# Third block's rows loaded first; low halves of w2 after the last indirect store; first expert weights loaded ahead of the expert stage

## The reference, cut to what matters

```python
h = _layernorm(x) * (1 + ca) + sa
x = x + ga * attention(h)              # causal; scores = tanh(qk) + two bias terms
h = _layernorm(x) * (1 + cb) + sb
logits = silu(h @ rw1 + rb1) @ rw2 + rb2
k_prob = softmax(top_k(logits, 2))
for e in range(8):
    out += we[:, None] * (silu(h @ w1[e] + b1[e]) @ w2[e] + b2[e])
x = x + gb * out
```

## Time and profile before

| | before |
|---|---|
| runs | 1859.3, 1864.91, 1857.8 us (median 1859.3) |
| profiled execution | 1861.52 us, of which the span of the instructions is 1859.6 us |
| busy, share of the span | PE 93%, DVE 70%, ACT 66%, POOL 33% |
| mean granted PE clock | 0.958 |
| DMA | 275.91 MB, mean 148 GB/s |

### The profile page before, as it was taken

The page is one execution under the profiler, slowest core; times in us unless marked ns, Lnnn a source line. Parts: engine busy times, 40 slices in busy tenths (PEclk is TensorE's granted clock), DMA queues, the critical chain, the costliest instruction groups (busy, mean ns, idle before and its releaser), DMA issues. The chain is left out here.

```text
span 1859.6 us, 35364 instructions
## 1 busy us (share of the span) xinstructions
PE 1730.3 (93%) x11140; PEld 1039.0 (56%) x11141; DVE 1309.9 (70%) x2675; ACT 1232.0 (66%) x1260; POOL 620.1 (33%) x715
## 2 busy tenths in 40 slices
PE   4689999999999999999999999899469999999997
PEld 1333434334334344334433334488369999999997
DVE  6457778878888888777877878544646666666664
ACT  1167889999999989989999999633413333333332
POOL 0645241532532553342240201246612222222222
PEclk8878999999999999999999999999779999999998
DMA  4586445667663295336674480272257777777773
GB/s 166 176 197 168 123 135 118 151 131 157 141 132 103 86 197 155 107 98 149 133 159 104 97 196 18 61 230 93 90 195 200 199 199 197 200 199 199 197 201 77
DMA packets 175370, 275.91 MB, mean 148 GB/s; under 512 B 20832, under 2 KB 105952, under 8 KB 173088
## 3 DMA queue, kind: packets, MB, share of 16 engines
q1 hardware_dynamic: 159904, 252.34, 50.6%
q0 software_dynamic: 13440, 17.97, 5.7%
q10 hardware_dynamic: 1920, 4.23, 0.7%
HBM read 205.51 MB, written 68.96 MB: 148 GB/s over the span
## 5 line engine op out<-in xcount | busy, mean ns | idle before, releaser
L1341 DVE SCALAR_TENSOR_TENSOR probs<-probs,scal,bil_ps 128x512 f32<-128x512 f32 (+1 forms) x1152 | 789.6, 715 | 237.8 <-PE bil_ps L1183 193.3
L1262 ACT ACTIVATE probs<-probs 128x2048 f32<-128x2048 f32 (+1 forms) x288 | 522.5, 1814 | 80.8 <-DVE probs L1341 80.1
L1255 ACT ACTIVATE probs<-raw_ps 128x2048 f32<-128x2048 f32 (+1 forms) x288 | 509.3, 1768 | 31.5 <-PE raw_ps L1165 22.7
L1183 PE MATMUL bil_ps<-u_mv,w_st 50*128 50x512 f32 (+3 forms) x1280 | 468.0, 454 | 28.7 <-DVE probs L1341 17.1
L1183 PEld LDWEIGHTS bil_ps<-u_mv,w_st 50*128 50x128 f32 x1280 | 198.9, 187 | 511.5 <-DVE probs L1341 424.9
L2063 ACT ACTIVATE rows_sb<-fc_ps,b 128x128 f32<-128x128 f32 x576 | 161.0, 369 | 345.3 <-DVE hid_lo L2095 304.5
L1202 PE MATMUL o_ps<-probs,v_sb 128*32 128x512 f32 (+3 forms) x2560 | 299.8, 550 | 2.7 <-POOL probs L1012 2.6
L1165 PE MATMUL raw_ps<-q_mv,k_st 64*128 64x512 f32 (+3 forms) x1280 | 270.1, 394 | 6.5 <-DMA q_mv<-q_split 4.7
L2019 PE MATMUL fc_ps<-modrow,rows_sb 128*128 128x128 f32 x2304 | 270.9, 276 | 0.0
L2019 PEld LDWEIGHTS fc_ps<-modrow,rows_sb 128*128 128x128 f32 x2304 | 264.9, 193 | 0.0
L1992 POOL DMA_INDIRECT out<-modrow,token x72 | 125.4, 1741 | 379.1 <-DVE modrow L2128 373.4
(11 more groups left out here) (233 smaller groups left out, 1531.6 us busy)
## 6 DMA issues: line engine op xcount, KB each, us to landing
rows_sb<-in_w SPq DMA_DIRECT2D x72, 1024.0 KB, 4.9
q_mv<-q_split SPq DMA_DIRECT2D x128, 128.0 KB, 5.5
rows<-x_rows SPq DMA_DIRECT2D x72, 130.0 KB, 2.1
v_rows<-rows_sb SPq DMA_DIRECT2D x8, 1024.0 KB, 6.1
o_t<-o_sb SPq DMA_DIRECT2D x32, 256.0 KB, 6.6
k_st<-k_split SPq DMA_DIRECT2D x16, 512.0 KB, 8.3
k_st<-k_split SPq DMA_DIRECT2D x32, 256.0 KB, 10.8
v_sb<-v_rows SPq DMA_DIRECT2D x8, 1024.0 KB, 14.0
```

The source lines that it names most:

```text
L1183: mm = pe.matmul(bil_ps[:, hd % 2, column:column + width], codes(kt)[row:row + BIAS_ROWS, :], u_mv[row:row + BIAS_ROWS, p, hd // 2, query: ...
L1255: act.activation(probs[:, s % NBUF, :, first:BLK], raw_ps[:, :, first:BLK], ACT.Tanh).then_inc(tanh_ready, 1)
L1262: act.activation(scores, scores, ACT.Exp).then_inc(exp_ready, 1)
L1341: dve.scalar_tensor_tensor(scores, scores, scal[:, ALPHA:ALPHA + 1], bil_ps[:, hd % 2, first:BLK], ALU.mult, ALU.add).then_inc(sum_ready, 1)
```

## The change

It has three parts.

1. `load_rows(2)` becomes the first thing in SP's stream of the front stage.
2. Of the low halves of w2, only those of experts 0 and 3 stay after `place_rows(6)`. Those of 4, 1, 2 and 7 are done by DVE at the end of the router stage, behind a new semaphore `all_sent` that POOL raises after its last send. Those of 5 and 6 are done in the expert stage, in DVE's steps 0 and 1, behind the share of that step; PE waits for both (`w2_low`) before the first product with w2. The buffers w2_raw and w2_split are the same memory as before.
3. The w1 of the first tile is loaded by SP at the end of the router stage, once `tile_expert` is there, the first 16 sends have landed (their rows lie where w1 goes) and `all_sent` is raised. In the expert stage SP's step 0 loads only the rows, and SP's first six steps are written out ahead of its loop.

```diff
+            load_rows(2)
             for o in ("Q0", "Q1", "C", "L"):
                 store(0, o)
...
             load_values(0)
-            load_rows(2)
             load_keys(1)
...
+            sp.wait_ge(pads_ready, 2)
+            sp.wait_ge(tr_mm, 2)
+            sp.wait_ge(first_scattered, 16 * 2 * SLOTS)
+            sp.wait_ge(all_sent, 1)
+            e = sp.value_load(tile_expert[0:1, 0:1], min_val=0, max_val=E - 1)
+            src = a["w1"].rearrange("e (k p) n -> e p k n", p=P)[ds(e, 1), :, :, :]
+            sp.dma_start(rows_sb[:, 0:KC * HID].rearrange("p (k n) -> p k n", k=KC),
+                         src.rearrange("z p k n -> (z p) k n")).then_inc(w1_first, 16)
             sp.wait_ge(x1_stored, 16 * N_BLK)
...
-                                                rows_sb[:, tile * PAY:(tile + 1) * PAY], None).then_inc(scattered, 16)
+                                                rows_sb[:, tile * PAY:(tile + 1) * PAY], None
+                                                ).then_inc(first_scattered if n < 2 else scattered, 16)
...
                 scatter(n)
-            pool.wait_ge(scattered, 16 * NTILE * TOPK)
+            pool.sem_inc(all_sent, 1)
+            pool.wait_ge(first_scattered, 16 * 2 * SLOTS)
+            pool.wait_ge(scattered, 16 * (N_RBLK - 2) * SLOTS)
...
-                    for i, e in enumerate((0, 3, 4)):
+                    for i, e in enumerate((0, 3)):
                         dve.wait_ge(w2_hi_ready, i + 1)
                         low_half(e)
...
-            dve.tensor_copy(tile_expert[:, :], expert_f[:, :])
+            dve.tensor_copy(tile_expert[:, :], expert_f[:, :]).then_inc(pads_ready, 1)
...
-            for i, e in enumerate((1, 2, 7, 5, 6)):
-                dve.wait_ge(w2_hi_ready, 3 + i + 1)
+            dve.wait_ge(all_sent, 1)
+            dve.wait_ge(w2_hi_ready, E)
+            for e in (4, 1, 2, 7):
                 low_half(e)
...
-        w1_in = [sem(f"w1_in{p}") for p in range(WB)]
+        w1_in = [w1_first] + [sem(f"w1_in{p}") for p in range(1, WB)]
...
                     sp.dma_start(rows[:, u % 2, :], dram["x_rows"][ds(row, P), :]).then_inc(rows_in[u % 2], 16)
+                    if isinstance(m, int) and m == 0:
+                        return
...
-            skewed(sp, NET, 0, UNROLL, step)
+            skewed(sp, NET, 1, UNROLL, step)
...
                         pe.wait_ge(w2_in, 16 * (E + 1))
+                        pe.wait_ge(w2_low, 2)
...
                                       ).then_inc(meta_ready, 1)
+                    if isinstance(m, int) and m < 2:
+                        part = ds((5 + m) * W2E, W2E)
+                        dve.tensor_tensor(w2_split[:, 1, part], w2_raw[:, part], w2_split[:, 0, part].bitcast(F32),
+                                          ALU.subtract).then_inc(w2_low, 1)
```

More of the change, by code:

```diff
@@ L315, in build @@
             pass
-        with nc.sbuf_tensor("w2_place", [P, E * HID // P * D], F32, side="right"):
+        with nc.sbuf_tensor("w2_raw", [P, E * HID // P * D], F32, side="right") as w2_raw:
             with nc.sbuf_tensor("rw1_hi", [P, KC * HID], F32R, side="right") as rw1_hi:
@@ L336, in build @@
                             rw1_hi, rw1_lo, x1_stored, h2_back, out)
[L337 to L340, removed]
+            w2_low = ctx.enter_context(nc.semaphore("w2_low"))
+            w1_first = ctx.enter_context(nc.semaphore("w1_first"))
+            stage_router(nc, a, dram, modrow, ident, rows_sb, w2_raw, w2_split, w2_in, out, wo, den, ln, rw1_hi, rw1_lo,
+                         tile_expert, expert_f, tile_row, x1_stored, h2_back, w1_first)
+        stage_experts(nc, a, dram, modrow, ident, rows_sb, tile_expert, expert_f, tile_row, w2_raw, w2_split, w2_in, w2_low,
+                      w1_first, out)
 HAM, SCALE, ALPHA, BETA, SIG_HAM, SIG_SCALE, HALF_LAM, LAT_SCALE, INV_BETA, ROOM = range(10)
@@ L1419, in skewed, with stage_router @@
         emit(m, m, lambda k: 0 <= m - k < total)
-def stage_router(nc, a, dram, modrow, ident, rows_sb, w2_split, w2_in, out, wo, den, ln, rw1_hi, rw1_lo,
-                 tile_expert, expert_f, tile_row, x1_stored, h2_back):
+def stage_router(nc, a, dram, modrow, ident, rows_sb, w2_raw, w2_split, w2_in, out, wo, den, ln, rw1_hi, rw1_lo,
+                 tile_expert, expert_f, tile_row, x1_stored, h2_back, w1_first):
     with ExitStack() as ctx:
@@ L1434, in stage_router @@
         right = lambda n, s, dt=F32: ctx.enter_context(nc.sbuf_tensor(n, s, dt, side="right"))
-        w2_raw = right("w2_raw", [P, E * HID // P * D])
+        right("w2_place", [P, E * HID // P * D])
         right("rw1_place", [P, KC * HID])
@@ L1442, in stage_router @@
         normed = inv_w.rearrange("p k (z d) -> p (k z) d", d=D)
-        w2_hi_ready, w2_lo_ready = sem("w2_hi_ready"), sem("w2_lo_ready")
+        w2_hi_ready, first_scattered, all_sent = sem("w2_hi_ready"), sem("first_scattered"), sem("all_sent")
         w2_part = lambda e: ds(e * HC * D, HC * D)
@@ L1749, in low_half @@
                 dve.tensor_tensor(w2_split[:, 1, w2_part(e)], w2_raw[:, w2_part(e)],
-                                  w2_split[:, 0, w2_part(e)].bitcast(F32), ALU.subtract).then_inc(w2_lo_ready, 1)
+                                  w2_split[:, 0, w2_part(e)].bitcast(F32), ALU.subtract)
             def split_rows(n):
@@ L1908, in _, with stage_experts @@
             dve.tensor_scalar(tile_row[:, :], row_f[:, :], float(VOID), None, ALU.min)
-            for i, e in enumerate((1, 2, 7, 5, 6)):
-                dve.wait_ge(w2_hi_ready, 3 + i + 1)
+            dve.wait_ge(all_sent, 1)
+            dve.wait_ge(w2_hi_ready, E)
+            for e in (4, 1, 2, 7):
                 low_half(e)
-def stage_experts(nc, a, dram, modrow, ident, rows_sb, tile_expert, expert_f, tile_row, w2_split, w2_in,
-                  out):
+def stage_experts(nc, a, dram, modrow, ident, rows_sb, tile_expert, expert_f, tile_row, w2_raw, w2_split, w2_in, w2_low,
+                  w1_first, out):
     with ExitStack() as ctx:
```

## The result

The changed kernel took 1851.55 us in the median of 6 runs (1849.67 to 1852.51), the kernel before, on the same chip, 1861.12 (6 runs, 1857.8 to 1864.91). The ratio is 0.9948, 95% interval [0.9935, 0.9961]: 9.6 us less. The profiled execution took 1851.5 us, of which the span is 1849.8 at a mean granted clock of 0.960; before, the span was 1859.6 at 0.958. The forecast was 10.7 less; as a median it was 1848.6 us, because it started from the three runs of before, with their median of 1859.3.

A forecast was written before the change was run, and what follows sets the result against it. PE bounds the kernel nearly everywhere, so only its idle places can pay: 4.7 + 3.5 + 2.5 = 10.7 us less, 1850.8 against the profiled 1861.52, as a median 1848.6; range 1843 to 1856.

The forecast's parts named there:

- Part 1, rows of block 2: Start of the attention steps: the mask wait of 2.58 us goes and queries come 2.1 earlier, 4.7 us less.
- Rival (c): Start of the attention steps: a later DMA wait replaces the mask, gain only 0 to 2.6 us; chance 0.10.
- Part 2, low halves: End of the router stage: sends free of low halves take 0.96 us, next stage starts at 1353.1, 3.5 us less.
- the new wait: End of the router stage: DVE waits for `all_sent`, then four low halves, 0.1 + 8.9 us, end at 1352.8.
- The side case, that `all_sent` is raised before the last send is through: End of the router stage: a low half beside the last send makes it take up to 2.75 us; nothing changes.
- The other chain: End of the router stage: landing of the last send, 7.28 us from its end to the next stage, giving 1351.1.
- The side case that w1's 1 MB holds the landing up: End of the router stage: w1's transfer delays the landing by 4.3 us, next stage at 1355.4, only 1.2 less.
- Part 3, first weights: Start of the expert stage: second tile's rows no longer wait behind w1, 2.5 us less, between 1.3 and 2.7.
- (a): Router stage's end: the 5.9 us gap hangs on the low halves and reopens; 5.1 less in total; chance 0.18.
- (b): End of the router stage: low halves do not slow the sends; 5.2 us less in total; chance 0.05.
- (d): Attention steps: more stretches at 1.2 GHz, 3 us each; four more turn the gain to a 1.3 loss; chance 0.05.

The follow-up runs named there:

- tail-only kernel: The changed kernel with load_rows(2) back in its old place, so parts 2 and 3 alone: 1854.07 us, ratio to before 0.9973.
- true wait: The changed kernel with all_sent raised by a small memset on POOL behind the last send, not by its queue: 1848.34 us, ratio to before 0.9943.
- two at start: The true wait kernel with only low halves 4 and 1 behind the last send, 2 and 7 at the experts' DVE start: 1845.46 us, ratio to before 0.992.

## Why the prediction was right, and where it was not

The forecast was 10.7 less and 9.6 came, within the range. Two terms were off, in opposite directions in the profile, and partly made up for each other: that the sum came within 1.1 us is in part luck.

**Part 1, rows of block 2: forecast 4.7.** Each step named can be seen: issue hidden at 36.24, norm at 87.71 (forecast 87.98), mask at 96.79 (97.3), no mask wait, queries 4.5 us earlier (2.1 taken). The profile shows 7.13 at the first values product and 5.93 at the router stage. Of the 7.13, 2.91 were there before: the first bilinear product was already that much earlier (88.40 against 91.31). This is the chance of two executions: in the early shape that product stood at 88.98 to 91.31 in the four profiles with late rows and at 88.40 to 91.28 in the three with rows first. Over these seven the gain is 5.5 at the first values product. What the prediction did not see is that the one profile it had showed one of two shapes of the start. In the other, with TensorE at a clock near 0.6 from 70 to 82 us, ACT's store issues are last and the wait for the mask does not exist. The term is nearer 3.5 over executions, with single ones further apart than that. Rival (c), the gain absorbed, was met in part at the first values product of the late shape, though not for its reason: no DMA wait took the mask's place, but a wait for ACT. At the router stage no run shows it.

**Part 2, low halves: forecast 3.5, measured 1.2 in the profile, 1.5 by the tail-only kernel.** The step that failed is the wait: "the new wait: DVE waits for `all_sent`, and four low halves are queued behind it". The side case, that `all_sent` is raised before the last send is through, is what happened, and it was mis-sized: priced with one low half beside one send, "nothing changes". It was raised with ten sends to come, and when the low halves began five were left, of which four took 4.4 us more together (8.28 against four times 0.96). The forecast had the sends end 5.5 us earlier; with these 4.4 still there, the sequence became only 1.5 shorter (27.10 against 28.60). With a true wait the same stretch is 3.77 shorter, as the 3.5 forecast had it, with the next stage 0.34 behind DVE (0.31 taken). The other chain was right in its size, 7.28 behind the last send forecast and 7.35 measured, but not in its name: of the 7.35 the landing is 1.5 and POOL's DRAIN 5.28. The side case that w1's 1 MB holds the landing up did not come: with two at start, where w1 was issued at 1341.71, 0.9 behind the last send's end, the gap was 7.38.

**Part 3, first weights: forecast 2.5, measured 2.9 in the profile and 2.8 alone.** The two row loads are issued within 1.55 us, where 2.64 lay between their starts, and the upper bound of 2.7 was reached and a little passed: PE no longer waits for the second rows, but 0.67 for DVE. The low halves in steps 0 and 1 (2.29 and 2.28 us) cost nothing visible: PE's first w2 product came 9.52 us behind the first product, against 9.16 before, and that product itself took 5.97 against 5.62.

**The rivals.** (a) would be named by a gap of 5 us or more behind the last low half, and there was one, of 9.44. The sign misled: the low halves had ended early, and the gap behind the last send was the same as before. What refutes (a) is the true wait, with 0.34 us and POOL's DRAIN running beside the low halves. That POOL has closing work of some 5 us was right in it. (b) is refuted by sixteen sends of 0.96. (d): the mean clock stayed at 0.960, and the window 214 to 220 us that ran at 0.50 ran at 0.94 this time; in the thirteen profiles this window stands anywhere from 0.50 to 1.00, and no mean clock was below 0.958.

## What to carry to other kernels

An increment in an engine's queue behind its sends can be up long before they have run, here by ten sends of sixteen; where work must stay off their time, raise the signal from an instruction of the engine itself that stands behind them, and look in the trace whether the waiting engine really waited. A wait seen in one profile of a program's start is one sample: before pricing its removal, look whether the stretch ahead of it has the same clock in other executions, and take the gain as a mean over the shapes. Where two chains end a stage, shorten both by the same amount: here low halves moved out of the stage paid only until POOL's chain, 7.3 us behind the last send, was later. And before a gap with no traffic is put down to a late landing, look at what the sequencers do in it: here 5.3 us of it were one engine's closing instruction.

## What the runs showed of the hardware

- A semaphore incremented in POOL's queue behind sixteen indirect stores was up at 1325.0 us, when ten of them had not begun; the last ended at 1342.09. One raised by a memset behind them came when they were through: DVE went on at 1338.97, 0.14 after the memset began.
- A vector subtraction of 128x2048 with both inputs and the output in SBUF holds an indirect store's issue on POOL: 0.96 us becomes 1.89 to 2.79. Without them sixteen sends took 19.96 us, with them 28.60.
- The wait for the landing of the indirect stores was over 1.5 us behind the last send's end with POOL waiting and 1.6 with SP waiting. POOL's closing DRAIN took 5.28 to 5.29 us behind that wait, and ended 5.4 us behind the last send where POOL did not wait for the landing. In the front stage, without sends, it took 0.73.
- The same program was granted 1.00 or 0.58 of the clock from 70 to 82 us in two executions, with PE busy 11.07 and 12.00 of 12 us, and its first score product moved by 5.8 us. What decides between the two stays open.
